# Summing the first head's exponentials on GpSimd and packing high and low values into one 128-column weight

## The reference

```python
kv = jnp.concatenate([xn @ Wkv, ln @ Wkv], axis=1)
qn = rmsnorm(q, qn_g) * scale
kn = rmsnorm(k, kn_g)
sim = jnp.einsum('bhid,bhjd->bhij', qn, kn)
attn = jax.nn.softmax(sim.astype(jnp.float32), axis=-1).astype(sim.dtype)
out = jnp.einsum('bhij,bhjd->bhid', attn, v)
```

## Time and profile before

| | us |
|---|---|
| device time, median of 3 runs | 2646.66 (2644.13 to 2647.74) |
| the profiled execution's own time | 2644.76 |
| its span, first to last instruction | 2643.1 |
| PE busy | 2502.3 (95%) |
| DVE busy | 1857.7 (70%) |
| ACT busy | 1691.6 (64%) |
| POOL busy | 1312.2 (50%) |

### The profile page before, as it was taken

How to read it: one execution, slowest core, us unless ns; L and a number is a source line. 1 busy time by engine, 2 the same in 40 slices (tenths; PEclk the granted TensorE clock), 3 DMA queues, 4 the chain that set the end, 5 groups by cost and what they waited for, 6 DMA issues and landing times. The chain is left out here.

```text
span 2643.1 us, 45087 instructions
## 1 busy us (share of the span) xinstructions
PE 2502.3 (95%) x14568; PEld 2048.0 (77%) x14568; DVE 1857.7 (70%) x2507; ACT 1691.6 (64%) x2286; POOL 1312.2 (50%) x784
## 2 busy tenths in 40 slices
PE   3699999999999999999999999986989999999998
PEld 3577777777777777777777777754989999999997
DVE  6666776767777777677677767765877557776775
ACT  2477777777777777778778777774332334454453
POOL 4344553555444544454445544541542526666675
PEclk8799999999999999999999999998989999999999
DMA  5665556545664566455655565545741449999996
GB/s 186 193 159 141 155 156 165 152 134 167 165 157 133 161 162 169 131 169 151 163 148 142 162 166 149 137 131 122 169 122 55 141 145 319 321 321 321 325 320 176
DMA packets 256912, 466.62 MB, mean 177 GB/s; under 512 B 65575, under 2 KB 145755, under 8 KB 251848
## 3 DMA queue, kind: packets, MB, share of 16 engines
q1 hardware_dynamic: 230166, 406.54, 54.6%
q0 software_dynamic: 25696, 58.82, 7.9%
q10 hardware_dynamic: 978, 0.34, 0.1%
HBM read 280.90 MB, written 79.85 MB: 136 GB/s over the span
## 5 line engine op out<-in xcount | busy, mean ns | idle before, releaser
L664 DVE TENSOR_TENSOR pr_lo<-pr,pr_hi 128x1024 fp32r<-128x1024 f32 x576 | 818.5, 1429 | 356.1 <-ACT pr_hi L765 350.6
L764 ACT ACTIVATE pr<-ps_s 128x1024 f32<-128x1024 f32 x512 | 525.9, 1027 | 332.9 <-PE ps_s L883 313.5
L765 ACT ACTIVATE pr_hi<-ps_s 128x1024 fp32r<-128x1024 f32 x512 | 522.1, 1020 | 0.0
L897 PE MATMUL ps_o<-pr_hi,vA 128*65 128x512 f32 x1152 | 464.9, 404 | 20.6 <-DVE o_second L603 11.3
L410 POOL TENSOR_TENSOR sq<-raw 128x1024 f32<-128x1024 f32 (+1 forms) x96 | 183.6, 1913 | 584.6 <-ACT raw L719 584.6
L899 PE MATMUL ps_o<-pr_lo,vA 128*65 128x512 f32 x1152 | 455.1, 395 | 0.0
L898 PE MATMUL ps_o<-pr_hi,vC 128*65 128x512 f32 x1152 | 453.2, 393 | 0.0
L1547 ACT ACTIVATE ht<-f_ps_h,b 128x256 f32<-128x256 f32 x440 | 184.6, 470 | 339.7 <-PE f_ps_h L1479 339.6
L414 POOL TENSOR_TENSOR rs<-ss,minus_half 128x16 f32<-128x16 f32 (+1 forms) x96 | 261.0, 2719 | 246.0 <-DVE ss L649 246.0
L883 PE MATMUL ps_s<-qq_hi,kk 128*128 128x512 f32 x1152 | 362.8, 396 | 8.2 <-ACT pr_hi L765 6.6
L883 PE MATMUL ps_s<-qq_lo,kk 128*128 128x512 f32 x1152 | 361.7, 395 | 0.0
(11 more groups left out here) (195 smaller groups left out, 3857.0 us busy)
## 6 DMA issues: line engine op xcount, KB each, us to landing
w<-w1S_dram SPq DMA_DIRECT2D x160, 512.0 KB, 6.0
lnT_sb<-lnT_dram SPq DMA_DIRECT2D x31, 2304.0 KB, 8.5
w2raw<-in_L_ffn_Wproj SPq DMA_DIRECT2D x78, 512.0 KB, 6.9
qq_hi<-q_hi SPq DMA_DIRECT2D x128, 256.0 KB, 4.8
qq_lo<-q_lo SPq DMA_DIRECT2D x128, 256.0 KB, 5.0
kk<-k_hi SPq DMA_DIRECT2D x64, 288.0 KB, 5.1
kk<-k_lo SPq DMA_DIRECT2D x64, 288.0 KB, 5.4
w1S_dram<-cut POOLq DMA_DIRECT2D x36, 512.0 KB, 4.2
```

Source lines behind the costliest of these rows:

```text
L664: v.tensor_tensor(pr_lo[:, d % RING, :], pr[:, d % 2, :], pr_hi[:, d % RING, :].bitcast(F32), ALU.subtract).then_inc(s_lo, 1)
L764: act.activation(pr[:, d % 2, :], ps_s[:, d % 2, :], ACT.Exp, bias=bias)
L765: act.activation(pr_hi[:, d % RING, :], ps_s[:, d % 2, :], ACT.Exp, bias=bias).then_inc(s_exp, 1)
L897: mm(out, upper, pr_hi[:, r, cols], start=k == 0, stop=False)
```

## The change

For the first head of each pair, on the path that the flag chooses here:

- `vA` and `vC` become one tile `vv` with, for each key tile and head, 64 columns of lower part, 64 of upper part and the ones. The two products with `pr_hi` become one with all 128 columns: lower x upper lands in rows 0 to 63 of `ps_o`, upper x upper in rows 64 to 127. The product with `pr_lo` adds into rows 0 to 63. So four products a unit instead of six, and no row for the denominator.
- Unit 0's full exponential goes to a new tile `total`, and POOL adds the exponentials of units 1 to 8 to it (`add`, 8 additions of 128x1024, float32). ACT's exponential of unit d (3 to 10) now waits for the addition of unit d - 2, since that reads the `pr` slot too.
- PE sums `total` over the partitions with 8 one-column products with ones (`sums`, unit 12) into a bank of `ps_m`, and ACT copies them to `den`. The projection's tiles 5 to 8 change bank for it, and tile 5 waits for the copy of tile 4.
- ACT copies the upper rows of `ps_o` down (`lifted`, unit 10, two copies of 64x512), and DVE adds the lower rows to them in place of its own two copies.
- SP no longer spreads the first head's denominator through DRAM.
- On POOL, the last group's power and scaling move behind the next window's first addition (`normalise(w, GROUPS - 1, 1)`), the additions stand around the clearing DMA and `split1`, and `raw1`, now half as large, is loaded in halves. Small tiles share space.

The second head of each pair keeps its three products and its column of ones. The core of the diff:

```diff
+            def add(w, k):
+                pool.wait_ge(s_exp, w.n(UNITS, k + 1))
+                if k == 1:
+                    pool.wait_ge(s_lo, w.n(UNITS, 1))
+                else:
+                    pool.wait_ge(s_added, w.n(KT - 1, k - 1))
+                g.tensor_tensor(total[:, :], total[:, :], pr[:, k % 2, :], ALU.add).then_inc(s_added, 1)
+
+            def window(w, general):
+                adds = w.attend and not general
                 if w.proj and not w.turn:
                     lower_w(w.other, w.n(1, 4))
+                if adds:
+                    add(w, 1)
+                if w.turn:
+                    normalise(w, GROUPS - 1, 1)
+                if adds:
+                    add(w, 2)
+                    add(w, 3)
+                    add(w, 4)
                 if not isinstance(w.v, int):
                     clear(w)
+                if adds:
+                    add(w, 5)
+                    add(w, 6)
                 if w.attend:
                     split1(w.v, w.v + 1, w.s)
+                if adds:
+                    add(w, 7)
+                    add(w, 8)
+                if w.attend and w.s == 0:
+                    load1(fc_v[bass.ds(w.v, 1)], 1)
...
                 if w.proj:
                     for k in range(GROUPS):
-                        normalise(w, k)
+                        squared(w, k)
+                        if k + 1 < GROUPS:
+                            normalise(w, k)
...
+            def lifted(w):
+                for g in range(QB):
+                    half = slice(512 * g, 512 * g + 512)
+                    if g == 0:
+                        wait(act, s_store[0], w.n(16))
+                        act.wait_ge(s_pv0, w.n(2, 1))
+                    else:
+                        act.wait_ge(s_pv, w.n(UNITS, KT))
+                    act.activation(o_sb[0][0:DH, half], ps_o[DH:2 * DH, g, :], ACT.Copy).then_inc(s_up, 1)
...
                         wait(act, s_lo, w.n(UNITS, d - 1))
+                        if not general and d == 0:
+                            wait(act, s_sum, w.n(1))
+                        if not general and 3 <= d < KT + 2:
+                            act.wait_ge(s_added, w.n(KT - 1, d - 2))
...
+            def sums(w):
+                if w.proj:
+                    pe.wait_ge(s_raw, w.n(KT, 2 * KT + SUM_TILE - 1))
...
+                pe.wait_ge(s_added, w.n(KT - 1, KT - 1))
+                for k in range(NT):
+                    ins = mm(ps_m[:, SUM_TILE % 2, k:k + 1], total[:, :].rearrange("p (q k) -> p k q", k=NT)[:, k, :],
+                             ones[:, 0:1].bitcast(F32), start=True, stop=True)
+                ins.then_inc(s_sum, 1)
...
+                    if general or h == 1:
+                        out = ps_o[0:DH + 1, q, :]
+                        mm(out, upper, pr_hi[:, r, cols], start=k == 0, stop=False)
+                        mm(ps_o[0:DH, q, :], lower, pr_hi[:, r, cols], start=False, stop=False)
+                        ins = mm(out, upper, pr_lo[:, r, cols], start=False, stop=last)
+                    else:
+                        if not last:
+                            mm(ps_o[:, q, :], vv[:, slot, k, h, 0:2 * DH], pr_hi[:, r, cols], start=k == 0, stop=False)
+                        ins = mm(ps_o[0:DH, q, :], vv[:, slot, k, h, DH:2 * DH], pr_lo[:, r, cols], start=False, stop=False)
+                        if last:
+                            ins = mm(ps_o[:, q, :], vv[:, slot, k, h, 0:2 * DH], pr_hi[:, r, cols], start=False, stop=True)
```

More of the change, by code:

```diff
@@ L78 @@
 FIRST_TURN = 2
+SUM_TILE = 5
 FIRST_PROJ = FIRST_TURN + TURNS
@@ L182, in attention @@
         cz = rec[0:CTX, :].rearrange("p (b d) -> p b d", d=D)
-        full = raw1[:, :].rearrange("p (s n) -> p s n", s=2)
+        full = total[:, :].rearrange("p (s n) -> p s n", s=2)
         ps_s = t.ps("ps_s", [P, 2, N])
@@ L207, in attention, with probabilities, summing, bank_of @@
         block = ctx.enter_context(nc.Block())
+        def probabilities(d, general):
+            return total[:, :] if d == 0 and not general else pr[:, d % 2, :]
+        def summing(w, general):
+            return w.attend and not general
+        def bank_of(w, tile, general):
+            return (tile + (summing(w, general) and tile >= SUM_TILE)) % 2
         def half_of(b, h):
@@ L476, in pool_windows @@
                 pool.dma_start(out[TOKENS:, :].rearrange("(r p) d -> p r d", p=P), empty[:, :, 0:D]).then_inc(s_clear, 16)
-                windows(pool, window)
+                windows(pool, lambda w: window(w, general))
                 for k in range(2):
@@ L687, in dve_windows @@
                 after = Window(WINDOWS // 2, 0)
-                output(after, 1, 1)
+                output(after, 1, 1, general)
             either(dve, dve_windows)
@@ L716, in projected @@
                     act.wait_ge(s_job, tile + 1)
-                bank = tile % 2
+                bank = bank_of(w, tile, general)
                 lo = 0 if tile < NT else PW
@@ L782, in _ @@
                 scaled(0, j)
-            act.wait_ge(s_const, 6)
-            either(act, lambda general: windows(act, window))
+            act.wait_ge(s_const, 5)
+            either(act, lambda general: windows(act, lambda w: window(w, general)))
         @block.tensor
@@ L838, in turn, with project @@
                 ins.then_inc(s_job, 1)
-            def project(w, tile):
-                out = ps_m[:, tile % 2, :]
+            def project(w, tile, general):
+                out = ps_m[:, bank_of(w, tile, general), :]
                 if tile < 2:
@@ L844, in project @@
                         pe.wait_ge(s_tlo, w.n(TURNS, 2 * TURNS + tile - 1))
+                elif summing(w, general) and tile == SUM_TILE:
+                    pe.wait_ge(s_raw, w.n(KT, 2 * KT + tile))
                 else:
                     pe.wait_ge(s_raw, w.n(KT, 2 * KT + tile - 1))
+                    if summing(w, general) and tile == SUM_TILE + 1:
+                        pe.wait_ge(s_summed, w.n(1, 1))
                 if not w.turn and tile % 4 == 0:
@@ L917, in window @@
                             turn(w, d - FIRST_TURN)
+                        if summing(w, general) and d == FIRST_PROJ + SUM_TILE:
+                            sums(w)
                         if w.proj and FIRST_PROJ <= d < FIRST_PROJ + KT:
-                            project(w, d - FIRST_PROJ)
+                            project(w, d - FIRST_PROJ, general)
                         if isinstance(w.v, int) and w.v == -1:
```

225 lines of the change are left out of this document (124 added, 101 removed).

## The result

The kernel with the change takes 3154.5 us (median of 4 runs, 3151.8 to 3157.1) against 2645.7 for the kernel before: ratio 1.192 [1.190, 1.194], 19% slower. The prediction was 3020 with a range of 2740 to 3150, so its sign and main mechanism stand and its size doesn't: the result lies above the range.

What follows compares the result with a forecast made beforehand. The prediction took PE to bound the kernel, and POOL's additions, alternating with DVE, after the change. 32 x (11.5 + 0.5) = 384, less 8.5 for the stall, is +375.5 on 2644.8: 3020 us, range 2740 to 3150.

Steps and rivals of the forecast that it cites:

- The rest of the window: From unit 10 on: PE leads again; net 0.5 us later a window, with -0.3 and 3 as ends.
- What bounds the kernel: Exponentials of unit 1 to 10, before the change: PE sets the pace, busy 24.31 of 25.08 us; POOL 10.19.
- PE's gain of 0.46 us a unit: First head's units, six value products down to four: 4.1 us a window, 3.7 of it inside the stretch.
- POOL's addition, 2.45 us: Each 128x1024 addition in units 1 to 8: 2.45 us alone, 1.9 as lower end, 3.4 when held.
- Exclusion, exponential 10 later by 11.5 us: Units 1 to 10: POOL and DVE operations with two SBUF inputs exclude each other; 11.5 us a window, chance 0.66.
- a DVE subtraction of 1.23 us inside a POOL addition: Sign in the changed kernel's trace, units 1 to 8, that would show the forecast wrong.
- additions alone: Rival for the stretch: no mutual exclusion beyond what is seen by chance; +81 us, 2726, chance 0.14.
- The sums, 1.0 us: Unit 12: eight one-column products on PE take 1.0 us a window, with 0 and 4 us as ends.
- The clock: Rival for the stretch: PE's gaps drop the clock to the 1.2 GHz level; +128 us, 3150, chance 0.13.
- some 4 us later: The clock rival's claim for exponential 10, beyond the forecast's 36.5 us stretch, with PE's work at 38.5 us.
- The range: Whole kernel: 2740 to 3150 us overall; the exclusion forecast's own range 2880 to 3110.
- The stall of the earlier trace: Last window but one: DVE's wait for denominators from DRAM, with PE standing 8.53 us, goes; 8.5 us less.

Runs made afterwards that it cites:

- No additions, one sum: The changed kernel without POOL's eight additions and the waits for them, and with one column sum instead of eight: 2613.4 us, 0.988 of the kernel before.
- `lower_w` behind the scaling: The changed kernel without additions and with one column sum, `lower_w` moved back behind the scaling of the last group: 2591.7 us, 0.980 of the kernel before.
- The fills: The changed kernel with each POOL addition replaced by one or two memory fills that read nothing, sums left as they are: 2838.5 us, 1.072 of the kernel before.
- the additions on DVE: The changed kernel with the eight additions on DVE instead of POOL, each behind the subtraction of its unit: 2947.5 us, 1.114 of the kernel before.
- twice the scores: The changed kernel with the score products of units 3 to 6 issued twice: 3156.7 us, 1.193 of the kernel before.
- sums by blocks: The changed kernel with each column sum over 128 neighbouring columns of `total` instead of every eighth: 3037.9 us, 1.148 of the kernel before.

## Why the prediction was wrong

The step that failed is in "The rest of the window": "saves tile 8's 0.46 and pays 1.0 for the sums", net 0.5 us a window with 3 as its upper end. It measured 5.3: the sums take 3.74 us instead of 1.0, and the low clock behind them, a term put at nothing, costs 1.9. Point by point:

- *What bounds the kernel; PE's gain of 0.46 us a unit.* Right. Four products a unit stand in the trace, and the saving was idle time in the stretch. No additions, one sum shows that it would have been nearly so anyway: 0.7 of the 3.7 us come through there, 1.4 with `lower_w` behind the scaling. I had looked for the next engine in POOL only.
- *POOL's addition, 2.45 us.* Right for one alone: 2.35 is the shortest of 256, and 3.24 the median, where I had 3.4 for a held one.
- *Exclusion, exponential 10 later by 11.5 us.* Right in kind and nearly in size: 10.5. The fills take the reads of SBUF away and leave POOL busy, and most of the cost goes; the additions on DVE cost half. The sign that was to show the forecast wrong, "a DVE subtraction of 1.23 us inside a POOL addition", did appear, twice in each of 29 windows, and it was a badly chosen sign: the addition waited meanwhile. In detail: I let addition 1 follow both subtractions and end at t = 6.3. It ended at 7.5 (the exponentials of unit 1 end at 1221.21), since DVE's small operation, held by `lower_w`, and two copies came ahead of the subtractions; exponential 10 came at t = 35.4 instead of 36.6, so turns behind it were shorter than counted. The rival "additions alone" (2726) falls.
- *The sums, 1.0 us.* This is the mis-sized term. I read the earlier trace rows as eight products and they were four, each two instructions; I put down the stride in words and gave it no price. Sixteen instructions at 0.235 are 3.74 us.
- *The clock.* It was a rival for the stretch, and there it costs nothing (twice the scores). PE's work there did grow, to 29.3 us instead of 20.6, but within time that POOL took anyway. That this rival's 3150 lies next to the measured 3154 is luck: it put 4 us more than the forecast between exponentials 1 and 10, and there 1 us less than the forecast was measured. Its "some 4 us later" doesn't follow from its own numbers either (38.5 less 36.6 is 1.9, which gives 3081). I asked nowhere what sixteen products of one column do to the clock. Behind them it falls, and the project and six value products take 1.5 us more in the window shown (6 products 0.20 later each, the project 0.34 longer), 1.9 in the mean of windows 1 to 29 (15.36 against 13.4 where it doesn't fall). So 5.3 is 3.3 for the fourteen instructions beyond the first two and 1.9 for the clock; the saving of 0.46, these first two and the copies cancel (exponentials 10 to 13: 10.11 in no additions, one sum, against 10.08 before).
- *The range.* I let the sums' upper end of 4 us into a net with upper end 3. With 4 less 0.46 that end is 3.5, and the forecast's own range goes to 3127, which is still short. Only with the clock's 1.9 is it 5.4, and 3188.
- *The stall of the earlier trace rows*. Right: it went once, 9.9 us by the exponentials against 8.5.
- *The sum.* The forecast was +375.5, the spans differ by 508.1. Of the 132.6 missing, 109 are in windows 0 to 29 (30 x 12.0 against 469.3: 1 us a window too much for the additions, 4.8 too little for the sums), 18 in the last two, whose units 10 to 13 I didn't look at apart, and 5.4 outside.

## What to carry to other kernels

Before work moves to an idle engine, ask which of its operations read the same memory side as those of its neighbour: engines that exclude each other give less together than one alone (3.3 us a unit against 2.5), and the one that comes second can stand for very long (a cast of 0.64 us for 18.5). Count instructions, not calls, when a row gives a price, and price the access pattern by a row that has it. When an engine that sets the pace is relieved, walk the next two engines through the stretch before the gain is written down: here 3.7 us freed brought 0.7.

## What the runs showed of the hardware that was not expected

- A plain float32 product of one column is two instructions, and they come further apart with strided weights: 0.235 us with weights strided by eight floats (load 335 ns), 0.12 with contiguous ones (192 ns).
- Behind sixteen such instructions (3.74 us), without any idle time of PE, the granted clock goes to the 1.2 GHz level, and value products start 0.43 apart instead of 0.23: in all 32 windows with the additions, in 27 of 32 without. With two of them and no additions it doesn't in any. With contiguous weights (1.84 us for the sixteen) it doesn't in windows 0 to 29.
- The exclusion isn't fair. While an addition of POOL waited, DVE ran two subtractions unheld (2.34 us for both) and the addition took 5.80 us; with DVE's operations one behind the other a cast of POOL took 18.52 us instead of 0.64. In 4 of the 32 windows of sums by blocks exponential 3 came 4.9 us after 2 instead of 7.1, and the stretch took 35.3 instead of 37.3: who goes first isn't fixed.
- An operation of DVE on 128x2 elements with one tensor input, 0.17 us alone, takes 1.44 when it meets POOL's `lower_w`, so it isn't only operations with two SBUF inputs that are held.
